# A chain of adapters over couples of token tiles: where the 32 x 32 turns of the adapter product stand, and when the second tile's adapter rows are loaded

## What is computed

```
x = x + _L0_cond_ref(x, itok_B_0_7, L0_cond_W, L0_cond_Wr, L0_cond_A, L0_cond_B)   # dense product + gated top-2 experts of rank 16
x = x + _L1_cond_ref(x, itok_B_0_15, L1_cond_weights)                              # 64 x 64 mix of the rows of a batch element
x = x + _L2_cond_ref(x, L2_cond_A, L2_cond_B, itok_B_4_50)                         # adapter of rank 16, one of 64
x = x + _L3_cond_ref(x, itok_B_0_23, L3_cond_W, L3_cond_b, L3_cond_lora_As, L3_cond_lora_Bs)  # dense + bias + adapter, one of 32
```

## Time and profile before

| | us |
|---|---|
| median of 3 runs | 909.32 |
| lowest and highest | 906.81, 909.46 |
| profiled execution | 909.15 |
| its span | 907.4 |
| TensorE busy | 894.5 |
| VectorE busy | 584.5 |
| ScalarE busy | 346.0 |
| GpSimd busy | 237.9 |

### The profile page before, as it was taken

How to read it: one execution, slowest core, us unless ns; L and a number is a source line. 1 busy time by engine, 2 the same in 40 slices (tenths; PEclk the granted TensorE clock), 3 DMA queues, 4 the chain that set the end, 5 groups by cost and what they waited for, 6 DMA issues and landing times.

```text
span 907.4 us, 14951 instructions
## 1 busy us (share of the span) xinstructions
PE 894.5 (99%) x4726; PEld 791.7 (87%) x4726; DVE 584.5 (64%) x1575; ACT 346.0 (38%) x800; POOL 237.9 (26%) x379
## 2 busy tenths in 40 slices
PE   9999999999999999999999998999999999999997
PEld 7888888888888889899999997998998989989987
DVE  6554454454367427668678666787686687686786
ACT  5544333333334333343433433424424334334333
POOL 2010110010010013532522523415416325235240
PEclk9999999999999999999999999999999999999999
DMA  6988786999663564656665765666666567667665
GB/s 241 310 263 281 215 256 208 304 344 247 198 196 122 172 199 135 201 167 190 214 187 177 219 189 155 199 205 195 186 192 216 173 177 219 190 180 217 184 195 157
DMA packets 105604, 187.71 MB, mean 207 GB/s; under 512 B 15926, under 2 KB 66870, under 8 KB 105526
## 3 DMA queue, kind: packets, MB, share of 16 engines
q1 hardware_dynamic: 105526, 186.76, 67.1%
HBM read 143.20 MB, written 49.81 MB: 213 GB/s over the span
## 4 chain that ended last, share of the span: by engine, by line
PE 81%; DVE 5%; SPq 4%; DMA 4%; POOL 3%; issue 3%; ACT 1%; DVEq 0%; POOLq 0%
PE ps_o L1406 27%; PE ps_d L1432 14%; PE ps_w L1440 11%; PE ps_s L1406 9%; PE ps_d L1440 7%; PE ps_o L1453 4%; PE ps_d L1447 4%; DMA mdraw<-t 2%; PE ps_o L1464 2%; SPq L446 2%; PE ps_s L1470 1%; POOL stat_raw L719 1%; DMA stat_raw<-x 1%; POOL rows_raw L719 1%; PE ps_w L1447 1%
## 5 line engine op out<-in xcount | busy, mean ns | idle before, releaser
L1043 DVE TENSOR_TENSOR stat_lo<-stat_raw,stat_hi 128x1024 fp32r<-128x1024 f32 (+1 forms) x127 | 144.0, 1134 | 30.2 <-ACT stat_hi L774 27.9
L774 ACT ACTIVATE stat_hi<-stat_raw 128x1024 fp32r<-128x1024 f32 (+1 forms) x127 | 116.8, 933 | 23.5 <-POOL stat_raw L658 8.4
L1432 PE MATMUL ps_d<-w_hi,stat_hi 128*128 128x512 f32 x256 | 103.9, 406 | 0.0
L1432 PE MATMUL ps_d<-w_lo,stat_hi 128*128 128x512 f32 x256 | 101.8, 398 | 0.0
L1432 PE MATMUL ps_d<-w_hi,stat_lo 128*128 128x512 f32 x256 | 101.7, 397 | 0.0
L1406 PE MATMUL ps_o<-chunk_a_hi,stat_hi 128*128 128x512 f32 x216 | 84.4, 391 | 0.5 <-DVE stat_lo L1043 0.4
L1406 PE MATMUL ps_o<-chunk_a_hi,stat_lo 128*128 128x512 f32 x216 | 84.1, 389 | 0.0
L1406 PE MATMUL ps_o<-chunk_a_lo,stat_hi 128*128 128x512 f32 x216 | 84.0, 389 | 0.0
L683 POOL CAST w_hi<-mdraw 128x512 fp32r<-128x512 f32 x32 | 19.7, 615 | 211.0 <-DMA mdraw<-t 211.0
L658 POOL TENSOR_TENSOR stat_raw<-stat_raw,ident 128x128 f32<-128x128 f32 x40 | 23.1, 579 | 183.5 <-DMA stat_raw<-stat 183.5
L1406 PE MATMUL ps_o<-chunk_b_hi,stat_hi 128*128 128x512 f32 x152 | 59.1, 389 | 0.0
(11 more groups left out here) (223 smaller groups left out, 2285.7 us busy)
## 6 DMA issues: line engine op xcount, KB each, us to landing
up<-tu SPq DMA_DIRECT2D x124, 256.0 KB, 4.1
stat_raw<-stat SPq DMA_DIRECT2D x59, 512.0 KB, 4.3
mdraw<-t SPq DMA_DIRECT2D x128, 208.0 KB, 3.0
stat_raw<-x SPq DMA_DIRECT2D x32, 512.0 KB, 3.5
out<-outb SPq DMA_DIRECT2D x30, 512.0 KB, 5.4
t<-md_a SPq DMA_DIRECT2D x16, 576.0 KB, 6.0
rows_raw<-x SPq DMA_DIRECT2D x32, 256.0 KB, 3.7
chunk_a_raw<-mov SPq DMA_DIRECT2D x24, 256.0 KB, 5.6
```

The costliest lines, as they stand in the source:

```text
L774: return nc.scalar.activation(dst, src, ACT.Copy)
L1043: return nc.vector.tensor_tensor(out=dst, in0=src, in1=rounded.bitcast(F32), op=ALU.subtract)
L1432: last = nc.tensor.matmul(plain_bank(t)[:, 0:WCOLS], rows[a][:, k, :], w[c][:, k, :], start=k == 0 and m == 0, stop=k == KB - 1 and m == l ...
```

## The change

vsum gets two buffers, one for tile a and one for tile b. On VectorE, hidden_rows(a) goes from the front half of the couple to the rear half, behind Rb_raw, and hidden_rows(b) goes from behind La_raw to behind Rb_lo; both now stand between the last uses of that couple and mix_lo(a). On SyncE, the four index reads of tile b are made in the couple in front, between load_up2(b1) and load_up3(b1), and load_md of that tile is issued at the end of the couple in front, behind load_s4, instead of behind load_up2(a1) of its own couple. On ScalarE ud_hi(b) goes ahead of gate_exp(a), and h3_hi(a1) ahead of mix_hi(b1). In the last couple hidden_rows(a) follows the front half, hidden_rows(b) goes ahead of plain_lo(b), and La_lo behind mix_lo. The orders of TensorE and GpSimd stay.

```diff
@@ tiles @@
-        vsum = sb("vsum", [BR, BR])
+        vsum = [sb(f"vsum{n}", [BR, BR]) for n in range(2)]
@@ SyncE, step(j, back, fin) @@
                 if back:
                     load_up2(a1)
-                if not at(j, 0):
-                    choose(b)
-                    load_md(b)
                 if fin:
                     store_out(b2)
...
                 if back:
                     load_up2(b1)
+                choose(b + 2)
+                if back:
                     load_up3(b1)
                 load_s2(j + 1)
                 choose(a + 2)
...
                 load_x1(j + 1)
                 load_s4(j + 1)
+                load_md(b + 2)
@@ ScalarE, fore(j, back, fin) @@
                     h2_hi(a1)
+                ud_hi(b)
                 gate_exp(a)
-                ud_hi(b)
                 after_P1(j)
                 if back:
                     h2T_copy(a1)
+                    h3_hi(a1)
                     mix_hi(b1)
-                    h3_hi(a1)
                     h3T_copy(a1)
@@ VectorE, hidden_sum(t) and hidden_rows(t) @@
-                nc.vector.tensor_tensor(out=vsum[:, :], in0=vhi[:, :], in1=vlo[:, :], op=ALU.add).then_inc(dve_vsum, 1)
+                nc.vector.tensor_tensor(out=vsum[t % 2][:, :], in0=vhi[:, :], in1=vlo[:, :], op=ALU.add).then_inc(dve_vsum, 1)
...
-                both = vsum[:, :, None].to_broadcast([BR, BR, 2])
+                both = vsum[t % 2][:, :, None].to_broadcast([BR, BR, 2])
@@ VectorE, fore(j, back, fin) @@
                 gate(a)
                 s_lo(j, 0)
-                hidden_rows(a)
                 if back:
                     h3_lo(a1)
@@ VectorE, step(j, back, fin) @@
                 La_raw(j)
-                hidden_rows(b)
                 hgT_lo(b)
                 La_lo(j)
                 if back:
                     h2_lo(b1)
                 Rb_raw(j)
+                hidden_rows(a)
                 plain_lo(b)
                 Rb_lo(j)
+                hidden_rows(b)
                 mix_lo(a)
@@ VectorE, last(j) @@
                 fore(j, True, True)
+                hidden_rows(a)
                 add_bias(a1)
...
                 hgT_lo(b)
-                La_lo(j)
+                hidden_rows(b)
                 plain_lo(b)
                 mix_lo(TURN_B)
-                hidden_rows(b)
+                La_lo(j)
                 h3_lo(b1)
```

## The result

| | before | changed |
|---|---|---|
| median of 5 runs, us | 907.14 | 899.7 |
| lowest and highest | 906.09, 909.46 | 898.69, 901.66 |
| profiled execution | 909.15 | 900.0 |
| its span | 907.4 | 898.2 |

The changed kernel takes 0.992 of the time before, 95% interval 0.9899 to 0.9941: 7.4 us less by the medians, where 902.1 us had been forecast.

The account below looks back on a forecast made before the run. TensorE, busy 894.5 of 907.4 us, was taken as the bound, so only its stops could yield time. 909.15 less 11.0 gained plus 3.9 for held ends gave 902.1 us, range 897.0 to 907.0.

Parts of the forecast that it names:

- the middle stops: TensorE's waits at L1485 before h3_rows(a1), mid-couple, put down to hidden_rows(a) and late h3_hi(a1); 5.5 us.
- the one late load: Tile b's adapter rows late in one couple: 2.61 us idle at ranks2(a1), then lower clock; cost 4.5 us.
- hidden_rows(a) leaves the front half: VectorE's 1.52 us ahead of h3_lo(a1) moves, h3_hi(a1) swaps with mix_hi(b1); all stops at L1485 go, 5.5 us.
- The load issued 5 us sooner: SyncE's load_md(b) goes out behind the previous couple's last x rows; the ud_hi(b) and ranks2 waits go, 4.5 us.
- The passes on SyncE: Load issues and index reads passing other SyncE work stay hidden; out, up3 and mix 1 to 2 us sooner, no gain.
- The turns, 11.0 us in all: Whole loop: gain taken between 10.0 from the items and 11.4 from loop turn times, giving 898.2 us without new waits.
- The held ends, 3.9 us: Couple ends: GpSimd sums hold hidden_rows(b)'s last cast, then mix_lo; three ends of 14 at 1.3 us.
- mix_lo then meets the second sum: Couple's end: after the held last cast, mix_lo is held by GpSimd's next sum, costing TensorE 1.3 us.
- Rival 1: Couple ends: nothing is held, casts slip through or sums begin later; 898.2 us, chance 0.25.
- Rival 4: Before h3_rows(a1): h3_hi(a1) still comes late, half of the 5.5 us stays; 904.8 us, chance 0.08.
- Rival 2: Late rows of tile a + 2 hit ud_hi and ranks2(b1), or end stops lower the clock; 906.6 us, chance 0.14.
- Rival 3: All 14 couple ends held at last cast and mix_lo, 1.3 us each; slower, 916.4 us, chance 0.11.

Follow-up runs that it names:

- the turns alone: Kernel before with only VectorE's part: both hidden_rows at the couple's end, two vsum buffers; SyncE and ScalarE unchanged: 903.93 us, ratio 0.9976.
- the loads alone: Kernel before with only SyncE's part and ud_hi(b) ahead of gate_exp(a): 898.9 us, ratio 0.9912; again on another chip 899.32 us, 0.991.
- the kernel with one turn in front: Changed kernel, hidden_rows(a) behind the front half's last s_lo, hidden_rows(b) ahead of plain_lo(b): 898.74 us, ratio 0.9911; again 898.35 us, 0.990.
- the one with both turns behind Rb_lo: Changed kernel with hidden_rows(a) also moved behind Rb_lo, ahead of hidden_rows(b): 909.0 us, ratio 1.0017 to the kernel before.

## Why the prediction was right, and where its steps were not

**The total.** 902.1 us was forecast and 899.7 measured. Between the two profiled executions the sum can be held against its terms: the gain without new stops was 9.15 + 1.2 = 10.35 us where 11.0 stood, and the new stops 1.2 us where 3.9 stood. The range of 897 to 907 us also took in two rivals and half of a third, so that a time inside it tells little of the mechanism. The stops in the traces do, and by them two steps were wrong, the cause of the middle stops and the price of a held end. That the total still came out near is in part luck, since what the turns were credited with was brought by the loads, which were in the same change.

**The base.** I took the profiled execution, 909.15 us, as standing for the runs. It held the one late load, and stood 2 us above the median of five runs, 907.14. On the three later chips the same kernel had medians of 905.33, 907.35 and 908.1 us. The late load's 4.5 us are gained only in executions that have one, which may be why the two profiled executions differ by 9.15 us and the medians by 7.4. Only two traces of the kernel before exist, one with the late load and one without, so how often it comes stays open.

**hidden_rows(a) leaves the front half, 5.5 us.** All stops at L1485 in the middle are gone, as said. But the cause was put in the wrong place. I read what ran just ahead of h3_lo(a1), the seven small instructions of 1.52 us, and gave them the whole stop. The runs: the turns alone about 2 us; the loads alone all of it, with neither the turns nor the swap of h3_hi(a1) and mix_hi(b1). The turns together with that swap, and the loads as before, were not run; they may bring the 5.5 us as well, and then each cure alone is enough. In the trace of the turns alone VectorE's own work is done 1.3 us or more before the ask in every couple, which makes that likely, as an estimate. The rows that would have told stand in the same timeline four lines up, gsel at 1.29 us and gates at 0.66 under GpSimd's CASTs. h3_lo(a1) has two inputs, and the loads bring both forward (medians): VectorE's by 0.9 us, through the gate, and ScalarE's h3_hi(a1) by 2.1 us, through load_mix(b1) and mix_hi(b1). At the stop of couple 11, from which the item was read, ScalarE's was the last of the two, so that the turns without the swap would have gained nothing there. The sum of both items, 10.0, was right because together they name all the stops; it was wrong to give the one item to the turns and only the rest to the loads.

**The load issued 5 us sooner, 4.5 us.** The place (748.26, right behind the last x rows), the missing wait at ScalarE and the absence of a stop at ranks2 came as described. The item took in only the late load. The steady part, the 13 or 14 smaller stops, goes with SyncE's part of the change too.

**The passes on SyncE** cost nothing, as said: load_up2(a1) follows at 750.35 and no instruction of TensorE waits for it. But that the mix rows go out 1 to 2 us sooner was put down as "no cost and no gain". In the changed kernel the swap of h3_hi(a1) and mix_hi(b1) hides that gain; in the loads alone the sooner load_mix(b1) is what brings h3_hi(a1) forward, and where it is missing, with the load issued early and the index reads not hidden, 2.4 us of stops stay.

**The turns, 11.0 us in all.** Without new stops the time would be the 900.0 of the profiled execution less 1.2, 898.8, against 898.2 forecast; the kernel with one turn in front, without any stop, took 898.0 in its profiled execution.

**The held ends, 3.9 us.** This is the step that failed, and the term that was mis-sized: 1.2 us in the first trace, 0.3 and 3.3 in the other two. The forecast had 3 ends of 1.3 us; the traces have 6, 1 and 4 ends with a stop. Nine of these eleven stops are of 0.12 to 0.39 us, the other two of 0.80 and 1.95. At eight the last cast was held by the first sum, as told. At the other three, one in each trace, the cast slipped through and mix_lo alone was held, which the kernel before has too. A held cast takes up to 1.31 us instead of 0.18, so a cast from SBUF to SBUF is held as a two-input instruction is. The Trainium skill, page "SBUF — State Buffer", section "Who interferes with whom", says that casts can take the ports that VectorE shares with GpSimd. The trace agrees in that.

Wrong was "mix_lo then meets the second sum". The traces of the changed kernel and of the one with both turns behind Rb_lo have 24 ends, first couples included, at which the last cast was held by the first sum and mix_lo came right behind it. At 20 mix_lo went first, with 0.28 us, and the second sum took 1.41 to 1.43. At four mix_lo was held for 1.41 to 1.45 us: the end with the stop of 1.95 us, and the first couple in each of the three traces of the changed kernel. At these four the cast had begun 0.28 us behind the first sum; at the other 20 it began 0.02 to 0.23 or 0.53 to 1.04 us behind it. Why that distance decides isn't known, and no run set it on purpose. The first couple of the turns alone has a fifth such place, with the same 0.28 us and mix_lo held again. Mostly, then, a hold that comes after a hold is not paid a second time, and the slack of some 1.1 us at the end covers nearly all of the one that is paid.

**The rivals.** Rival 1, nothing held, 898.2, came nearer in time than the forecast, 1.5 us off against 2.4, but ends were held in all three traces. Rival 4, ScalarE's h3_hi too late, is ruled out by the 2.1 us of margin, though it is what limits the kernel with the turns alone. Rival 2 named the right load: the two ends at which GpSimd's CAST of the rows of tile a + 2 begins latest, 3.0 and 2.8 us ahead of plain(a), have the two largest stops, 0.80 and 1.95 us rather than 4.5. Among the others the rows don't decide alone: in the second trace two ends with 3.2 and 3.4 us have no stop. Rival 3 would have needed the second hold at each end.

## What to carry to other kernels

When an engine is late, read its durations further back than the instruction next to the stop: one that takes three times its usual time names the engine that held it, and that engine's own start may hang on a DMA. Ask for rows as soon as their buffer is free, and read the indices for them where the issuing queue waits anyway; here that alone brought 0.9%. Where the late instruction has two inputs, take the end of each against the time at which it is asked for; here both were late, and both through SyncE. Before pricing two changes that cure the same stops, ask what each would do alone, since the second may only add its cost.

## What the runs showed of the hardware

When a cast of VectorE had been held by a GpSimd sum and both engines had the next instruction ready, VectorE's went ahead at 20 of 24 such places, and GpSimd's 128x512 sum then took 1.42 instead of 1.29 us. The other four are those at which the cast had begun 0.28 us behind the sum. A held last cast ends 33 to 43 ns behind the instruction that held it, a held mix_lo 146 to 153 ns.

32 x 32 turns of VectorE in SBUF ran in their usual 0.85 us for four under a GpSimd sum, while the cast behind them was held by the same sum. All 128 of them take 199 to 207 ns each, in every trace. The prediction's sentence that a VectorE instruction whose operands all lie in SBUF is held while a GpSimd one runs is thus too wide.

An idle time of 1.79 us in front of h3_rows (a stop of 1.95 us) was not followed by a lower clock, the idle time of 2.61 us in front of ranks2 was. The windows view (busy time and number of instructions of each engine, granted clock, DMA share, GB/s) behind the stop of 1.95 us in the changed kernel; the window behind the other is the last of the earlier trace rows, with 0.66:

```profile
683.50:688.50 5.00, 5.00 (x30) 4.26 (x31) 4.86 (x7) 3.80 (x7) 2.65 (x3) 1.00 0.64 172
```
